# Two graph layers on one core: key and query columns projected together with the last head, 272 columns at once

## What is computed

```
h = relu(layernorm(x));  x = x + adj @ (h @ W0) + b0
h = relu(layernorm(x))
feat_proj = (h @ fc_w + fc_b), 8 heads of 256 columns
q = feat_proj @ q_w + q_b;  k = feat_proj @ k_w + k_b        (one number per node and head)
attn = softmax(leaky_relu(q + k^T + (1 - adj) * -1e9, 0.01))
y = concat_heads(attn @ feat_proj) @ fp_w + fp_b + h
x = x + sigmoid(y)
```

## Time and profile before

| | |
|---|---|
| median of 3 runs | 1406.27 us (1406.05 to 1407.6) |
| span of the profiled execution | 1404.9 us; its time beside the span is not given, the median of the runs is 1.4 us longer |
| granted TensorE clock | 1.000 over the whole span |
| PE busy | 1394.7 us, 99%, 9048 matmul issues |
| DVE busy | 1285.1 us, 91% |
| ACT busy | 1126.5 us, 80% |
| POOL busy | 1102.0 us, 78% |
| DMA | 124.69 MB, 177132 packets, of which 137808 under 512 B |

### The profile page before, as it was taken

How to read it: one execution, slowest core, us unless ns; L and a number is a source line. 1 busy time by engine, 2 the same in 40 slices (tenths; PEclk the granted TensorE clock), 3 DMA queues, 4 the chain that set the end, 5 groups by cost and what they waited for, 6 DMA issues and landing times.

```text
span 1404.9 us, 31603 instructions
## 1 busy us (share of the span) xinstructions
PE 1394.7 (99%) x9048; PEld 1252.5 (89%) x9048; DVE 1285.1 (91%) x4408; ACT 1126.5 (80%) x3429; POOL 1102.0 (78%) x1295
## 2 busy tenths in 40 slices
PE   9999999999999999999999999999999999999998
PEld 7898899899899889998998898998989989988987
DVE  7999999999999999999999999999999999998996
ACT  4878788788888888887888888888878878887876
POOL 4788878878778878778787788787787887888764
PEclk9999999999999999999999999999999999999999
DMA  7423323323223233233232232232332322322221
GB/s 238 98 63 107 107 54 106 91 69 106 71 88 106 55 105 106 54 105 97 63 106 80 79 106 61 99 106 54 105 103 58 106 88 73 106 67 85 77 61 41
DMA packets 177132, 124.69 MB, mean 89 GB/s; under 512 B 137808, under 2 KB 143568, under 8 KB 177104
## 3 DMA queue, kind: packets, MB, share of 16 engines
q1 hardware_dynamic: 176816, 124.35, 30.3%
q10 hardware_dynamic: 288, 0.01, 0.0%
HBM read 105.98 MB, written 18.35 MB: 89 GB/s over the span
## 4 chain that ended last, share of the span: by engine, by line
PE 94%; POOL 2%; issue 1%; DVE 1%; DMA 1%; ACT 0%; POOLq 0%; SPq 0%; ACTq 0%; DVEq 0%
PE gbank L381 48%; PE ybank L381 24%; PE tbank L481 8%; PE bank L381 6%; PE bank L426 4%; PE bank L462 2%; PE bank L449 2%; DMA late<-key_rows 0%; POOL att L1561 0%; POOL att L1554 0%; DMA qk<-qk_w_dram 0%; DVE att L829 0%; POOL xb L1544 0%; POOL t_pos L1546 0%; POOL ends L1577 0%
## 5 line engine op out<-in xcount | busy, mean ns | idle before, releaser
L1233 ACT ACTIVATE att<-att 128x128 f32<-128x128 f32 x1024 | 397.8, 393 | 47.0 <-DVE att L836 44.0
L381 PE MATMUL gbank<-m_hi,hT_lo 128*128 128x512 f32 x1024 | 426.7, 417 | 0.0
L1554 POOL TENSOR_TENSOR att<-late,t_pos 128x512 f32<-128x512 f32 x256 | 330.6, 1293 | 120.5 <-PE tbank L481 115.8
L381 PE MATMUL gbank<-m_hi,hT_hi 128*128 128x512 f32 x1024 | 403.2, 394 | 0.0
L381 PE MATMUL gbank<-m_lo,hT_hi 128*128 128x512 f32 x1024 | 401.3, 392 | 0.0
L812 DVE TENSOR_TENSOR g_lo<-gbank,g_hi 128x512 fp32r<-128x512 f32 x512 | 341.4, 678 | 47.1 <-ACT g_hi L1226 42.0
L1561 POOL TENSOR_TENSOR att<-att,rinv 128x512 f32<-128x512 f32 x256 | 289.4, 1131 | 107.1 <-DVE rinv L841 106.5
L1226 ACT ACTIVATE g_hi<-gbank 128x512 fp32r<-128x512 f32 x512 | 291.1, 595 | 39.6 <-PE gbank L381 39.4
L829 DVE TENSOR_SCALAR_CACHE_REDUCE att<-att,qs 128x128 f32<-128x128 f32 x1024 | 291.6, 341 | 27.0 <-POOL att L1554 26.7
L381 PE MATMUL ybank<-g_hi,pT_hi 128*128 128x256 f32 x1016 | 281.5, 277 | 0.0
L381 PE MATMUL ybank<-g_hi,pT_lo 128*128 128x256 f32 x1016 | 281.4, 277 | 0.0
(11 more groups left out here) (97 smaller groups left out, 2323.1 us busy)
## 6 DMA issues: line engine op xcount, KB each, us to landing
late<-key_rows SPq DMA_DIRECT2D x64, 1024.0 KB, 6.1
g_in<-graph_dram SPq DMA_DIRECT2D x64, 512.0 KB, 3.4
out_dram<-ends SPq DMA_DIRECT2D x63, 256.0 KB, 3.9
qs<-key_rows SPq DMA_DIRECT2D x128, 4.0 KB, 2.5
key_rows<-kq_sb SPq DMA_DIRECT2D x64, 24.0 KB, 1.4
att<-fc_wT_dram SPq DMA_DIRECT2D x4, 256.0 KB, 5.6
late<-fp_w_dram SPq DMA_DIRECT2D x4, 256.0 KB, 5.3
ends<-fp_w_dram SPq DMA_DIRECT2D x2, 512.0 KB, 7.9
```

Source lines behind the costliest of these rows:

```text
L381: mm = pe.matmul(out_ap, w, m, start=first and n == 0, stop=last and n == len(terms) - 1)
L1233: e = act.activation(a[:, s], a[:, s], ACT.Exp, scale=-1.0, bias=a[:, CH + h:CH + h + 1], accum_out=esum[j][c][:, h:h + 1])
L1554: gp.tensor_tensor(a, keys[q][:, j, c * HC:(c + 1) * HC, :], t_pos[q][:, j, :].unsqueeze(1).broadcast_to([P, HC, P]), ALU.add)\
```

## The change

The projection of a pair has nine pieces instead of eight and a key/query group. `A0, A1, A2` are heads 0 to 5 of graph 0, `B0, B1, B2` of graph 1, 512 columns each. `SIXTH` is head 6 of both graphs in one bank, 256 columns each, six matmuls for each graph. `HERE` and `THERE` are head 7 of graph 0 and of graph 1 with the 16 columns of u behind it, 272 columns, six matmuls each; they are made one step early, where queries_keys stood, HERE in bank1 and THERE in the ring. Keys and queries so come out with a node per partition.

```diff
-RING = ((7, -1), (1, 0), (2, 0), (3, 0), (0, 0), (4, 0), (6, 0), (5, 0))
+A0, A1, A2, B0, B1, B2, SIXTH = range(7)
+HERE, THERE = 7, 8
+LAST = (HERE, THERE)
+RING = ((B0, -1), (A1, 0), (A2, 0), (THERE, 1), (A0, 0), (SIXTH, 0), (B2, 0), (B1, 0))
+BEFORE = ((A0, A1), (A2, SIXTH, HERE)), ((B0, B1), (B2, SIXTH, THERE))
...
-            def queries_keys(p, q):
...
-                for dt in range(DT):
-                    for h in (hT_lo, hT_hi):
-                        mm = pe.matmul(kq.rearrange("r (j n) -> r j n", j=J), u[:, dt, :], h[q][:, dt, :, :],
-                                       start=dt == 0 and h is hT_lo, stop=dt == DT - 1 and h is hT_hi)
-                mm.then_inc(pe_kq, 1)
+            def last_head(p, q, j):
+                bank = here if j == 0 else ring_free(THERE, p)
+                folded(p)
+                split(bank[:, 0:WIDE],
+                      [((hT_hi[q][:, dt, j, :], hT_lo[q][:, dt, j, :]), (n_hi[:, dt, 0:WIDE], n_lo[:, dt, 0:WIDE]))
+                       for dt in range(DT)]).then_inc(pe_g[LAST[j]], 1)
...
+            def sixth_heads(p, q):
+                bank = ring_free(SIXTH, p)
+                folded(p)
+                s = slice(6 * D, 7 * D)
+                for j in range(J):
+                    mm = split(bank[:, j * D:(j + 1) * D],
+                               [((hT_hi[q][:, dt, j, :], hT_lo[q][:, dt, j, :]), (m_hi[:, dt, s], m_lo[:, dt, s]))
+                                for dt in range(DT)])
+                mm.then_inc(pe_g[SIXTH], 1)
...
             def step(i, q):
-                project(i - 1, (q + 2) % U, 7)
-                attend(i - 1, 0, 1)
+                project(i - 1, (q + 2) % U, B0)
+                attend(i - 1, (q + 2) % U, 0, 1)
                 transpose_h(i + 1, (q + 1) % U)
-                project(i, q, 1)
+                project(i, q, A1)
                 transpose_p(i - 1, 1, 1)
-                project(i, q, 2)
+                project(i, q, A2)
                 h_ready(i + 1)
-                queries_keys(i + 1, (q + 1) % U)
-                project(i, q, 3)
-                attend(i - 1, 1, 0)
-                project(i, q, 0)
+                last_head(i + 1, (q + 1) % U, 0)
+                last_head(i + 1, (q + 1) % U, 1)
+                attend(i - 1, (q + 2) % U, 1, 0)
+                project(i, q, A0)
...
-                project(i, q, 4)
-                project(i, q, 6)
+                sixth_heads(i, q)
+                project(i, q, B2)
```

`attend` waits for the pieces in `BEFORE` and takes head 7 from `last_hi` and `last_lo`, which have three buffers. ACT's `kq_rows` is gone and `last_high(p, q, j)` copies 256 columns of head 7. On DVE:

```diff
-            def keys_queries(p, q):
-                dve.wait_ge(a_kq, p + 1)
...
-                for j in range(J):
-                    s = slice(j * P, (j + 1) * P)
-                    r = dve.scalar_tensor_tensor(out=kq_sb[q][j * HALF:j * HALF + ROWS], in0=kq[0:ROWS, s],
-                                                 scalar=kq_bias[0:ROWS, 0:1], in1=kq_low[:, s], op0=ALU.add,
-                                                 op1=ALU.add)
-                r.then_inc(v_kq, 1)
+            def keys_queries(p, q, j):
+                dve.wait_ge(a_g[LAST[j]], p + 1)
...
+                dve.tensor_tensor(kq_sb[q][:, :, j, :], last_bank(j, p)[:, D:WIDE].rearrange("p (k h) -> p k h", k=2),
+                                  kq_bias[:].rearrange("p (k h) -> p k h", k=2), ALU.add).then_inc(v_kq[j], 1)
+
+            def last_low(p, q, j):
+                dve.wait_ge(a_g[LAST[j]], p + 1)
+                dve.tensor_tensor(last_lo[q][:, j, :], last_bank(j, p)[:, 0:D], last_hi[q][:, j, :].bitcast(F32),
+                                  ALU.subtract).then_inc(v_g[LAST[j]], 1)
...
-                keys_queries(i + 1, (q + 1) % U)
+                keys_queries(i + 1, (q + 1) % U, 0)
+                last_low(i + 1, (q + 1) % U, 0)
                 inverse(i, 0, 0)
                 leaky(i, 0, 1)
+                keys_queries(i + 1, (q + 1) % U, 1)
                 pT_low(i - 1, 1, 1)
```

`last_low(i + 1, 1)` stands where g_low of piece 3 stood, and SIXTH, A0 to B2 take the places of the pieces they follow from (SIXTH that of piece 4). `mask_min` reads the queries from `kq_sb`. `queries_in` is gone from SP's lists, and the store of the keys transposes:

```diff
             def keys_out(p, q):
-                sp.wait_ge(v_kq, p + 1)
+                for j in range(J):
+                    sp.wait_ge(v_kq[j], p + 1)
                 if has(p - 1):
                     sp.wait_ge(s_rows, 16 * p)
-                sp.dma_start(key_rows[q][0:HALF + ROWS], kq_sb[q][0:HALF + ROWS]).then_inc(s_rows, 16)
...
+                sp.dma_start(key_rows[q].rearrange("r n -> n r"), kq_sb[q][:, 0, :, :].rearrange("p j h -> p (j h)"),
+                             allow_slow_non_contiguous=True).then_inc(s_rows, 16)
```

More of the change, by code:

```diff
@@ L82, in gnn_pair @@
         w0_hi, w0_lo = sb("w0_hi", [P, DT, D], F32R, LINE), sb("w0_lo", [P, DT, D], F32R, LINE)
[L83 to L89, removed]
+        m_hi, m_lo = sb("m_hi", [P, DT, (H - 1) * D], F32R, LINE), sb("m_lo", [P, DT, (H - 1) * D], F32R, LINE)
+        g_hi, g_lo = sb("g_hi", [P, J, (H - 1) * D], F32R, LINE), sb("g_lo", [P, J, (H - 1) * D], F32R, LINE)
+        last_hi, last_lo = three("last_hi", [P, J, D], F32R, LINE), three("last_lo", [P, J, D], F32R, LINE)
+        ident = sb("ident", [P, P], F32, LINE)
+        n_hi, n_lo = sb("n_hi", [P, DT, PITCH], F32R, LINE), sb("n_lo", [P, DT, PITCH], F32R, LINE)
         b0_row = sb("b0_row", [P, D])
-        none = sb("none", [P, DT, 2 * HALF])
         qk = sb("qk", [P, DT, 2])
-        kqb = sb("kqb", [P, 1])
-        kq_bias = sb("kq_bias", [P, 1])
+        kqb = sb("kqb", [P, 2])
+        kq_bias = sb("kq_bias", [P, ROWS])
         c_row = sb("c_row", [P, D])
         b_part, b_sum, b_rows = sb("b_part", [P, DT, H, 2]), sb("b_sum", [P, H, 2]), sb("b_rows", [P, ROWS])
-        c_part = sb("c_part", [P, D])
         ones = sb("ones", [P, P])
@@ L183, in adjT_of, with m_at, u_at, g_at @@
             return g_in[q][:, J * D + J * P:].rearrange("p (j n) -> p j n", j=J)
-        def u_at(dt, h, at):
-            return u[:, dt, at:at + ROWS].rearrange("p (k h) -> p h k", k=2)[:, h, :]
+        def m_at(m, n, dt, h):
+            return m[:, dt, h * D:(h + 1) * D] if h < H - 1 else n[:, dt, 0:D]
+        def u_at(n, dt, h):
+            return n[:, dt, D:WIDE].rearrange("p (k h) -> p h k", k=2)[:, h, :]
+        def g_at(g, last, q, j, h):
+            return g[:, j, h * D:(h + 1) * D] if h < H - 1 else last[q][:, j, :]
+        def piece(g, n):
+            if n == SIXTH:
+                return g[:, :, 6 * D:7 * D]
+            return g[:, n // 3, n % 3 * BANK:(n % 3 + 1) * BANK]
+        def bank_of(n, p):
+            bank = gbank[tenant(RING, RSIZE, n, p)[0]]
+            return bank[:].rearrange("p (j d) -> p j d", j=J) if n == SIXTH else bank[:]
+        def last_bank(j, p):
+            return here if j == 0 else gbank[tenant(RING, RSIZE, THERE, p)[0]]
         def steady(eng, step, first, last):
@@ L406, in key_query_bias @@
                 pe.wait_ge(v_bias, 4)
-                pe.matmul(ybank[0:ROWS, 0:2], b_rows[:], ones[:, 0:2], start=True, stop=True).then_inc(pe_bias, 1)
+                pe.matmul(ybank[:, 0:ROWS], ones[:], b_rows[:], start=True, stop=True).then_inc(pe_bias, 1)
             def output_bias():
@@ L411, in output_bias @@
                 pe.wait_ge(v_cpart, H * DT)
-                pe.matmul(ybank[:, 0:D], ones[:], c_part[:], start=True, stop=True).then_inc(pe_crow, 1)
+                pe.matmul(ybank[:, 0:D], ones[:], c_part, start=True, stop=True).then_inc(pe_crow, 1)
             def ring_free(n, p):
@@ L442, in transpose_h @@
                 if has(p - 1):
[L443 removed]
+                    pe.wait_ge(v_g[HERE], p)
                     pe.wait_ge(v_hTlo, p)
@@ L967, in begin @@
                 pT_low(1, 0, 1)
-                g_low(1, 5)
-                g_low(1, 4)
+                g_low(1, SIXTH)
+                g_low(1, B1)
                 inverse(1, 1, 1)
@@ L1039, in step @@
                 stats0(i + 3, q)
-                g_low(i - 1, 4)
+                g_low(i - 1, SIXTH)
                 mean0(i + 3, q)
@@ L1185, in load_bias @@
                 act.dma_start(fcb[:], fc_b).then_inc(s_small, 16)
-            def u_none():
-                act.wait_ge(g_none, 1)
-                act.activation(u[:], none[:], ACT.Copy).then_inc(a_none, 1)
             def w0_high():
```

609 lines of the change are left out of this document (294 added, 315 removed).

## The result

The changed kernel takes 1913.27 us in the median (1905.13 to 1914.44), against 1406.4 us: ratio 1.3588, interval [1.3562, 1.3614]. The prediction said 1379.5 us, faster. The profiled execution spans 1911.6 us at a mean granted clock of 0.892, where it was 1.000.

What follows compares the result with a forecast made beforehand. PE's steps were taken to bound the kernel: profiled span 1404.9 us, minus 26.8 saved on PE, plus 1.4 around a span, gives 1379.5 us, faster by 1.9%; own range 1373 to 1388 us.

Steps and rivals of the forecast that it cites:

- What bounds the kernel: Steady loop: PE is busy for all 300 us from 400 to 700 at full clock, so its start-to-start steps set time.
- PE per pair: Projection and key/query matmuls on PE: 2.812 us added, 3.23 removed, net -0.418 us a pair, 26.8 us in all.
- Rival 4: Matmuls hold the longer 0.1183 us step throughout because waits have come near: 1386.9 us; no separate chance, inside the forecast's 0.72.
- Other engines, and who is late next: DVE -0.17 and ACT -0.22 us a pair, POOL unchanged; nobody becomes late for PE, so its whole saving is hidden.
- Rival 1: DVE takes over: period falls only by its 0.17 us, 1395.4 us, or grows by 0.14, 1415 us; chance 0.15.
- Keys and queries: Two query loads go; the transposing key store takes 2.5 to 3.5 us, within 4.2 us available, and costs nothing.
- rival 2: Scattered key store is slow: 6.8 us free, each us beyond costs every pair 1 us; e.g. 1469 us; chance 0.08.
- PE's 0.8: Last part of the key store's slack: pT_lo ready 0.8 us before attention half (1,1) after the change.
- Head and tail: First and last pairs: some 0.7 us late at the end against 0.4 to 0.6 won at the start; taken as nothing.
- Rival 3: The 272-column matmul is priced as the 512-column one, 0.230 us: 1463.4 us; chance 0.04.

Runs made afterwards that it cites:

- the two runs with waits: Changed kernel with 64 B key runs, one wait per attention half: 1407.59 us; kernel before with two satisfied waits added per half: 1407.21 us.
- the runs kernel: Changed kernel with the key store writing one 64 B run per node instead of 16 scattered elements, keys in wrong order: 1407.79 us, ratio 1.0008.

## Why the prediction was wrong, by its steps

**What bounds the kernel.** Right: without the slow store PE has no idle time from 400 to 700 us, and its steps set the period.

**PE per pair.** Right in sign, too large. 272 columns: 0.124 and 0.127 us a step for 0.1208, +0.05 us a pair. That 512 columns and two 256-column steps cost the same held for head 6. The term that fell is one that the sum did not have: the four halves of attention, not touched by the edit, take 0.208 us more a pair, 13.3 us over 64. Rival 4 had the longer step of 0.1183, but only for the 24 new matmuls and for a cause (waits near) that the two runs with waits exclude. The row it came from, 1.42 us at 1375.12, was misread as one where PE had just been held: PE is busy in all 6.50 us from 1370 to 1376.5. Of 0.418 us a pair 0.155 came.

**Other engines, and who is late next.** Right in the steady loop: in the runs kernel DVE is busy for 274.9 of 300 us (277.7 before), and no new wait holds PE. Rival 1 did not happen.

**Keys and queries.** This step failed, and with it the sign. "I take 2.5 to 3.5" priced a write of 4 B by the row of a read. The read was right as far as it goes, 2.9 us for 2,048 elements; the write takes 11.7 by itself, and in the kernel the key load goes out 11.6 behind it. "From above nothing here bounds it" stood in the text, and yet the chance of rival 2 was put at 0.08 because its break-even lay at five times the read, as if the read bounded the write. The issue times were right: 4.04 us from key store to key load, predicted 4.2. The slack behind it was right in size too: 2.6 us taken, 3.0 seen in the runs kernel. Two of its three parts are the waits it named: the keys ahead of the mask (0.5 taken, 0.8 seen) and the mask ahead of DVE's read (1.3, 1.25). The third, PE's 0.8, was taken from the half (1,1); the path goes through the g_lo of B2 to A2, with 0.96, so that it fits there is luck. The step that failed is the price of the store.

**Rival 2.** Right in mechanism, with the signs it had named (POOL at the key load, SP held at keys_in), and right in what is free: keys 6.8 + 6.1 = 12.9 us behind the store by its working, 13.0 seen. Wrong in three sizes. The store: 8.2 us taken, 11.6 seen. The key load behind it: 6.1 taken, 7.7 seen. And each us beyond "costs every pair 1 us" leaves out the slow stretch from A2 to the keys, 2.2 us a pair. By the rival's law 11.6 - 6.8 - 0.42 = 4.4 us a pair would have been 1404.9 + 1.4 + 64 x 4.4 = 1688 us, and it is 1913, 7.8 us a pair. Of the 3.4 between them 1.6 are the load, 2.2 the slow stretch and 0.3 the gain that did not come, less 0.7 that passes quicker elsewhere in the loop. Why the key load takes longer stays open: in the kernel before with the store added the graph load lands as late (11.1 us in the median), and the key load takes 6.2 us in the mean.

**Head and tail.** "Both at nothing, within 1 us" was wrong. By the starts of the key groups on PE, the runs kernel is 3.0 us behind the kernel before at pair 5, gains 8.3 from there to pair 59, and loses 7.3 in the last pairs: -5.3 becomes +2.0. I had looked at PE's last half alone, not at when pair 63's keys are made. In order, some 5 us of it come back.

**Rival 3.** 272 columns fall on the slope, within 5%.

## What to carry to other kernels

A read's price says nothing of a write's: where an edit brings a pattern that no row shows, measure that transfer alone, and give its unbounded side a real chance. When the layout turns, keep the DMA's innermost run long and let an engine with time to spare take the stride. When you add up slack along a chain, read each engine's list behind the delayed instruction: if it leads back to the producer, every us beyond the slack returns each round, and more than that where the stall lowers the clock. And a gain of 2% in matmul steps can be half lost to the placement of other tiles, so read the untouched groups too.

## What the runs showed of the hardware

- 2,048 writes of 4 B to DRAM: 11.7 us side by side, 4.4 us at 64 B or more apart; as pieces of 8, 16 and 64 B 4.6, 2.8 and 1.4 us. The number matters little (512 of them: 8.6 us). While such a store runs, the profile shows DMA engines at 0.00, and a load issued 3.4 us behind it needs 10.0 us instead of 3.4.
- Twelve 256-column matmuls take 1.36 or 1.42 us, uniformly within the group. A shift by 32 B of tiles that are not the group's operands turns half of attention's groups from one to the other in the kernel before and a quarter back in the runs kernel, by their place in the period. The cause is open: it is not the waits, not the clock (1.00 in both), and not the place of g. That other engines' or DMAs' accesses to SBUF meet PE's reads would fit, but no run shows it.
- A POOL operation of 128x512 elements with one operand at a step of 64 B takes 1.56 instead of 1.30 us.
